# Two stacked transformer blocks on one core: three kinds of 16-bit turns by transposing transfers instead of TensorE

## What is computed

```python
xn = _layernorm(x)
x = x + L0_attn(xn, Wq, bq, Wk, bk, Wv, bv, Wo, bo) + L0_ffn(xn, w_gating, w_linear)
xn = _layernorm(x)
x = x + L1_attn(xn, wq, wk, wv, wo, inv_freq) + L1_ffn(xn, w_gate_up, w_proj)
# L0_attn: 32 query heads of width 8, 8 key/value heads, rotary, causal over the 1024 rows
# L0_ffn:  gelu(xn8 @ Wg0) * (xn8 @ Wg1), then @ w_linear, operands rounded to 8-bit floats
# L1_attn: rotary, softmax over the 16 heads of one row (each row by itself)
# L1_ffn:  ternary-quantized weights, silu(gate) * up, rms_norm, then @ w_proj
```

## Time and profile before

| | us |
|---|---|
| median of 3 runs | 600.06 |
| lowest, highest | 599.37, 602.33 |
| profiled execution: span, first to last instruction | 601.7 |
| profiled execution: its own time | not given, only the span is |
| TensorE, ScalarE, VectorE, GpSimd busy | 562.0, 469.6, 426.6, 233.6 |
| mean granted TensorE clock, share of full | 0.983 |

### The profile page before, as it was taken

The page is one execution under the profiler, slowest core; times in us unless marked ns, Lnnn a source line. Parts: engine busy times, 40 slices in busy tenths (PEclk is TensorE's granted clock), DMA queues, the critical chain, the costliest instruction groups (busy, mean ns, idle before and its releaser), DMA issues. The chain is left out here.

```text
span 601.7 us, 13300 instructions
## 1 busy us (share of the span) xinstructions
PE 562.0 (93%) x5153; PEld 290.7 (48%) x5153; DVE 426.6 (71%) x909; ACT 469.6 (78%) x607; POOL 233.6 (39%) x302
## 2 busy tenths in 40 slices
...
GB/s 265 303 36 2 36 1 35 36 2 49 6 62 33 33 59 39 27 37 3 19 17 2 64 54 27 89 55 27 54 10 36 45 20 69 17 68 85 94 57 48
DMA packets 150914, 30.40 MB, mean 51 GB/s; under 512 B 133952, under 2 KB 149568, under 8 KB 150848
## 3 DMA queue, kind: packets, MB, share of 16 engines
q1 hardware_dynamic: 150272, 29.19, 24.4%
q10 hardware_dynamic: 576, 0.33, 0.3%
...
## 5 line engine op out<-in xcount | busy, mean ns | idle before, releaser
L958 ACT ACTIVATE Pt<-psS 128x1024 f32<-128x1024 f32 x288 | 281.7, 1047 | 44.8 <-PE psS L685 25.9
L699 PE MATMUL psV<-Pt,vaug 128*32 128x512 f32 x1152 | 150.3, 611 | 0.3 <-POOL Pt L1645 0.3
L1645 POOL TENSOR_SCALAR_AFFINE_SELECT Pt<-Pt 128x1024 f32<-128x1024 f32 x64 | 71.7, 1145 | 43.8 <-ACT Pt L958 43.8
L685 PE MATMUL psS<-qTf,kTf 32*128 32x512 f16 x576 | 74.9, 390 | 7.3 <-ACT Pt L958 3.7
L685 PEld LDWEIGHTS psS<-qTf,kTf 32*128 32x128 f16 x576 | 20.3, 91 | 82.9 <-ACT Pt L958 48.1
L1695 POOL TENSOR_TENSOR ss<-ss,mhalf 128x1 f32<-128x1 f32 x16 | 9.5, 596 | 111.3 <-DVE ss L1476 111.3
L699 PEld LDWEIGHTS psV<-Pt,vaug 128*32 128x32 f32 x1152 | 25.7, 109 | 41.9 <-issue 35.9
L1016 ACT ACTIVATE stage<-psS 128x1024 f32<-128x1024 f32 x32 | 31.0, 1020 | 8.1 <-PE psS L821 7.9
L1686 POOL TENSOR_TENSOR r<-qk,cos 128x256 f32<-128x256 f32 x16 | 11.9, 744 | 63.9 <-ACT qk L991 58.0
L866 PE MATMUL psB<-wguT,xhs 128*128 128x512 bf16 x108 | 27.8, 380 | 0.0
L1032 ACT ACTIVATE qtmp<-qtmp 128x1024 bf16<-128x1024 f32 x16 | 16.9, 1059 | 12.9 <-PE psA L876 8.4
...
## 6 DMA issues: line engine op xcount, KB each, us to landing
qkvscr<-rqkv SPq DMA_DIRECT2D x16, 384.0 KB, 2.5
G<-qkvscr SPq DMA_DIRECT2D x24, 128.0 KB, 3.7
stage<-in_wg SPq DMA_DIRECT2D x4, 512.0 KB, 8.8
w8g<-qkvscr SPq DMA_DIRECT2D x16, 128.0 KB, 3.8
oscr<-o SPq DMA_DIRECT2D x16, 128.0 KB, 3.3
at<-oscr SPq DMA_DIRECT2D x16, 128.0 KB, 2.0
out<-yout SPq DMA_DIRECT2D x16, 128.0 KB, 2.5
...
```

Source lines behind the costliest of these rows:

```text
L685: e.matmul(psS[j], kd[32 * j:32 * j + k, h, 128 * at:128 * at + 128], qd[32 * j:32 * j + k, 4 * h:4 * h + 4, :].rearrange("p s n -> p (s n ...
L699: ins = e.matmul(psV[32 * j:32 * j + 32, :], vaug[:, at, j, 32 * h:32 * h + 32], Pt[(4 * Q + j) % NP], start=(kb == 0 and h == 0), stop=(k ...
L958: e.activation(flat(Pt4[:, u % NP:u % NP + 2, :]), flat(psS4[:, j:j + 2, :]), ACT.Exp, scale=scale).then_inc(S["exp"], 1)
L1645: e.affine_select(out=p, in_=p, pattern=[[0, 8], [1, 128]], compare_op=ALU.is_ge, fill=0.0, base=0, channel_multiplier=-1).then_inc(S["mas ...
```

## The change

`qxT`, `kTc`, `qTc`, `hxT`, `hTc` go, and `xn1T`, `xn1Tc` go from the first pass. Four transposing transfers on SP's queue replace them, from SBUF to SBUF: `kt`, `qt` (out of `QX`), `ht` (out of `hx_b`) and `xt`. For `xt` the split into a 16-bit part and its remainder is made ahead of the turn: a new VectorE step `xs` writes both into `xs_b`, memory that the first pass did not use. The steps that waited for a turn on TensorE or a copy on VectorE wait for a landing instead. The five lists of `ORDER` are all new (only SP's is shown); PSUM banks follow from TensorE's list.

```diff
     "sp": (
-        "wt.2 wg.2 wg.3 wg.4 wg.5 wt.3 wt.4 wt.5 vw.0 vr.0 vw.1 vr.1 ow.0 at1r.0 vw.2 vr.2 vw.3 ow.1 at1r.1 out.0 "
...
-        "at1r.12 vw.15 out.11 ow.13 vr.15 at1r.13 ow.14 out.12 at1r.14 ow.15 at1r.15 out.13 out.14 out.15"),
+        "wg.2 wg.3 qt.0 kt.0 qt.1 kt.1 wg.4 qt.2 wg.5 kt.2 qt.3 wt.2 kt.3 wt.3 qt.4 wt.4 xt.0 wt.5 kt.4 qt.5 xt.1 vw.0 "
+        "kt.5 kt.6 vr.0 qt.6 ht.0 xt.2 vw.1 xt.3 vr.1 ow.0 at1r.0 vw.2 vr.2 ht.1 qt.7 kt.7 ow.1 vw.3 at1r.1 vr.3 xt.4 "
...
+        "at1r.10 vw.12 vr.12 ht.11 xt.14 ow.11 vw.13 at1r.11 vr.13 ht.12 xt.15 vw.14 out.10 ow.12 vr.14 at1r.12 vw.15 "
+        "ow.13 vr.15 at1r.13 out.11 ht.13 ow.14 ht.14 out.12 out.13 at1r.14 ow.15 at1r.15 ht.15 out.14 out.15"),
...
+        xs_b = [flat(b[:]).bitcast(F16) for b in xn1T_b]
...
+            def kt(n):
+                at = n % NT % RING
+                w.wait_ge("q0", n + 1)
+                w.wait_ge("kl", n + 1)
+                w.wait_ge("pv", keys_free(n))
+                e.dma_start_transpose(kT[:, :, 128 * at:128 * at + 128],
+                                      QX[n % len(QX)][:, 32:40, :].rearrange("p h c -> p (h c)")).then_inc(S[f"d_kt{n % 2}"], 16)
+
+            def qt(n):
+                w.wait_ge("qh", n + 1)
+                w.wait_ge("ql", n + 1)
+                if n >= len(qT):
+                    w.wait_ge("qk", 4 * QUAD_END[n - len(qT)])
+                e.dma_start_transpose(qT[n % len(qT)],
+                                      QX[n % len(QX)][:, 0:32, :].rearrange("p h c -> p (h c)")).then_inc(S[f"d_qt{n % 2}"], 16)
+
+            def xt(n):
+                dst = xhs[n % len(xhs)]
+                w.wait_ge("xs", 2 * n + 2)
+                w.wait_ge("qkv1", 2 * (n + 1 - len(xhs)))
+                w.wait_ge("gu", 4 * (n + 1 - len(xhs)))
+                e.dma_start_transpose(dst[:].rearrange("p a (c n) -> p (a c) n", n=128),
+                                      xs_b[n % len(xs_b)]).then_inc(S[f"d_xt{n % 2}"], 16)
+
+            def ht(n):
+                w.wait_ge("hxa", n + 1)
+                w.wait_ge("hx", n + 1)
+                w.wait_ge("dn1", n)
+                w.wait_ge("wsum", 2)
+                e.dma_start_transpose(hT.rearrange("p k s n -> p (k s) n"),
+                                      hx_b.rearrange("p k n -> p (k n)")).then_inc(S["d_ht"], 16)
...
             def qk(Q):
-                    w.wait_ge("kTc", n - n % NB + kb + 1)
-                    w.wait_ge("qTc", n + 1)
+                    key = n - n % NB + kb
+                    w.wait_ge(f"d_kt{key % 2}", 16 * (key // 2 + 1))
+                    w.wait_ge(f"d_qt{n % 2}", 16 * (n // 2 + 1))
...
             def dn1(n):
-                w.wait_ge("hTc", 2 * n + 2)
+                w.wait_ge("d_ht", 16 * (n + 1))
...
             def qh(n):
-                    w.wait_ge("qxT", 2 * (n + 1 - len(QX)))
+                    w.wait_ge(f"d_qt{n % 2}", 16 * (n // 2))
...
             def ssq(n):
-                w.wait_ge("hxT", 2 * n)
+                w.wait_ge("d_ht", 16 * n)
...
+            def xs(n):
+                src, dst = xn1_b[n % len(xn1_b)], xs_b[n % len(xs_b)]
+                w.wait_ge("xn1", n + 1)
+                w.wait_ge(f"d_xt{n % 2}", 16 * (n // 2))
+                e.tensor_copy(dst[:, 0:256], src[:]).then_inc(S["xs"], 1)
+                w.wait_ge("xs", 2 * n + 1)
+                e.tensor_tensor(dst[:, 256:512], src[:], dst[:, 0:256], ALU.subtract).then_inc(S["xs"], 1)
```

More of the change, by code:

```diff
@@ L49 @@
     "pe": (
[48 rows of a table removed]
-    "act": (
[26 rows of a table removed]
-    "dve": (
[42 rows of a table removed]
-    "pool": (
[16 rows of a table removed]
[41 rows of a table added]
+    "act": (
[25 rows of a table added]
+    "dve": (
[37 rows of a table added]
+    "pool": (
[19 rows of a table added]
 }
 ROUND = {
[3 rows of a table removed]
[2 rows of a table added]
     "act": "qh QUADS g:0 fh:0 sq:0 th:0 g:1 fh:1 sq:1 th:1 qk1c gTk ex1 tg:0 tg:1 ssq hxa",
[5 rows of a table removed]
[4 rows of a table added]
 }
-PARTS = {"qxT": 2, "fxT": 3, "fTc": 3, "mT": 2, "up": 4, "qkv1": 2, "gT": 2, "gu": 4, "hxT": 2, "sq": 2, "fh": 2, "th": 2,
+PARTS = {"fxT": 3, "fTc": 3, "mT": 2, "up": 4, "qkv1": 2, "gT": 2, "gu": 4, "sq": 2, "fh": 2, "th": 2,
          "tg": 2, "mTc": 2, "g": 2, "ge1": 2, "ge3": 2, "sg": 2,
-         "hh": 2, "hTc": 2, "ge4": 2}
-ROUND2 = {e: r.replace("qxT:0 qxT:1", "fxT:0 fxT:1 fxT:2 rmm mT:0 mT:1").replace(" kl kTc qTc", " fTc:0 fTc:1 fTc:2 rmax mTc:0 mTc:1")
-          .replace(" ql", "").replace(" osum", "") for e, r in ROUND.items()}
+         "hh": 2, "ge4": 2}
 QUAD_STAGES = {"pe": ("qk", "pv"), "act": ("exp",), "pool": ("mask",)}
@@ L215, in one_round @@
     steps = []
-    for word in (ROUND if n < NT else ROUND2)[engine].split():
+    for word in ROUND[engine].split():
         if word == "QUADS":
@@ L236 @@
     "xnT": lambda n: ("xnTc", 2 * n + 2), "qkv": lambda n: ("qkvc", n + 1),
-    "qxT": lambda m: ("qTc" if m % 2 else "kTc", m // 2 + 1), "fxT": lambda m: ("fTc", m - 3 * NT + 1),
+    "fxT": lambda m: ("fTc", m - 3 * NT + 1),
     "mT": lambda m: ("mTc", m - 2 * NT + 1), "obT": lambda n: ("att", 2 * n + 2), "attT": lambda n: ("attTc", n + 1),
     "wo0": lambda n: ("xa", n + 1), "up": lambda m: ("fh" if m % 2 else "g", m // 2 + 1), "down": lambda n: ("yff", n + 1), "flagT": lambda n: ("flag", 1), "wsum": lambda m: ("wmin", m + 1),
-    "xn1T": lambda n: ("xn1Tc", 2 * n + 2) if n < NT else ("xn1f", n - NT + 1), "qkv1": lambda m: ("v1c" if m % 2 else "qk1c", m // 2 + 1),
+    "xn1T": lambda n: ("xn1f", n - NT + 1), "qkv1": lambda m: ("v1c" if m % 2 else "qk1c", m // 2 + 1),
     "gT": lambda m: ("gTk" if m % 2 else "gTq", m // 2 + 1), "gTagain": lambda n: ("gTm", n - NT + 1),
@@ L243 @@
     "o1T": lambda n: ("o1", 2 * n + 2), "at1T": lambda n: ("at1Tc", n + 1), "wo1": lambda n: ("yo", n + 1),
-    "gu": lambda m: ("hh" if m % 2 else "sg", m // 2 + 1), "hxT": lambda m: ("hTc", m + 1), "dn1": lambda n: ("yout", n + 1),
+    "gu": lambda m: ("hh" if m % 2 else "sg", m // 2 + 1), "dn1": lambda n: ("yout", n + 1),
     "ts": lambda m: ("tsc", m + 1), "td": lambda m: ("tde", m + 1), "tr": lambda m: ("tw", m + 1),
@@ L265, in score_banks @@
     return dict(zip(fills[1:], fills))
-SEMS = """d_x0 d_x1 d_x2 d_id d_b d_cs d_w0 d_c d_w1 d_wg0 d_wg1 d_gu0 d_gu1 d_vw0 d_vw1 d_vr d_ow d_or d_out0 d_out1
-xnT qkv qxT fxT mT obT attT wo0 up down xn1T qkv1 gT S1m gTagain S1 PV1 o1T at1T wo1 gu hxT dn1 ts td tr qk pv rmm flagT
+SEMS = """d_ht d_kt0 d_kt1 d_qt0 d_qt1 d_xt0 d_xt1 d_x0 d_x1 d_x2 d_id d_b d_cs d_w0 d_c d_w1 d_wg0 d_wg1 d_gu0 d_gu1 d_vw0 d_vw1 d_vr d_ow d_or d_out0 d_out1
+xnT qkv fxT mT obT attT wo0 up down xn1T qkv1 gT S1m gTagain S1 PV1 o1T at1T wo1 gu dn1 ts td tr qk pv rmm flagT
 qh exp g sq fh th qk1c gTk ex1 tg ssq hxa tc tde sin
-idc vz tab cst w8 w8m w8s tsc tm tcs tw ln0 xn xnTc qkvc va wide q0 kl kTc qTc fTc rmax rcomb mxn mTc ob att attTc xa ge1 ge3 ge3b a8c yff
-wh wsq wsum ln1 xn1 xn1Tc xn1f wl wmin v1c ro1 ro2 gTq m1 gTm o1r o1 sg hh ssm hx hTc at1Tc yo yout osum flag rng rngb
+idc vz tab cst w8 w8m w8s tsc tm tcs tw ln0 xn xnTc qkvc va wide q0 kl xs fTc rmax rcomb mxn mTc ob att attTc xa ge1 ge3 ge3b a8c yff
+wh wsq wsum ln1 xn1 xn1Tc xn1f wl wmin v1c ro1 ro2 gTq m1 gTm o1r o1 sg hh ssm hx at1Tc yo yout osum flag rng rngb
 zero gz zf rs0 rope ql mask ge4 xf rs1 ro1p rsg w8a""".split()
@@ L546, in all_landed @@
                 w.wait_ge("d_or", 16 * NT * passes)
-            run = {"wg": wg, "wt": wt, "vw": vw, "vr": vr, "ow": ow, "at1r": at1r, "out": out}
+                w.wait_ge("d_ht", 16 * NT * passes)
+            run = {"wg": wg, "wt": wt, "vw": vw, "vr": vr, "ow": ow, "at1r": at1r, "out": out, "kt": kt, "qt": qt, "xt": xt, "ht": ht}
             load_first()
@@ L626, in qkv @@
                 e.matmul(bank[:, 0:384], src[:, 1, :], wqkv[:, 1, :], start=False, stop=True).then_inc(S["qkv"], 1)
-            def qxT(m):
-                n, part = divmod(m, 2)
-                src = QX[n % len(QX)]
-                w.wait_ge("idc", 2)
-                w.wait_ge("q0", n + 1)
-                w.wait_ge("kl", n + 1)
-                if part == 1:
-                    w.wait_ge("qh", n + 1)
-                    w.wait_ge("ql", n + 1)
-                bank = shared("qxT", m)[:].bitcast(F16).rearrange("p (s n) -> p s n", n=128)
-                for at, u in enumerate(range(8) if part else range(8, 10)):
-                    ins = e.transpose(bank[:, at, :], src[:, 4 * u:4 * u + 4, :].rearrange("p r c -> p (r c)"), identh[:])
-                ins.then_inc(S["qxT"], 1)
             def transpose_heads(bank, units, sem):
@@ L769, in qkv1 @@
                     src = xhs[n % len(xhs)]
-                    w.wait_ge("xn1Tc", 2 * n + 2)
+                    w.wait_ge(f"d_xt{n % 2}", 16 * (n // 2 + 1))
                     w.wait_ge("wh", 1)
@@ L859, in gu @@
                 src = xhs[n % len(xhs)]
-                w.wait_ge("xn1Tc", 2 * n + 2)
```

(42 more changed lines are left out.)

19 lines of the change are left out of this document (8 added, 11 removed), and 260 rows, old and new, of tables (ORDER, ROUND).

## The result

The kernel after takes **570.01 us** (median of 4 runs, 569.08 to 571.85), the kernel before 599.73 on the same chip: ratio **0.951 [0.948, 0.954]**. Forecast were 579 us and a range of 558 to 601; the gain is 30 us where 21 were forecast.

A forecast was written before the change was run, and what follows sets the result against it. TensorE's queue was taken as the bound, above all from 150 to 540 us. 601.7 - 25 (turns) - 1 (copies) - 1 (holding) + 3 (start) + 3 (tail) = 580.7, less 1.6: 579 us, range 558 to 601.

The forecast's parts named there:

- TensorE's turns: Turns removed from TensorE's queue: 27.4 us, less 2.4 for those before 150 us where TensorE is not always the bound.
- VectorE's copies: 37.6 us of copies removed from VectorE: worth nothing from 150 us on, 1 us from 60 to 150.
- the chain's price: What a batch of turns costs its successor on TensorE, 0.45 us for 8; all removed turns sum to 27.4 us.
- the busy price: Removed turns priced by TensorE's busy time instead, 42 us in all; kept as the other end.
- The order: The new order of all five queues, priced at nothing, within plus or minus 3 us.
- less holding beside GpSimd: VectorE operations held while GpSimd runs: 15 us estimated in all, covered by TensorE after 150 us, counted as 1 us.
- Start and tail: Added cost of first `qt`, `kt` landing behind loads, 3 us (-1 to 8), and of last `ht`, 3 us (0 to 8).
- The rival in which they become the bound: Transposing transfers in 32-byte pieces fill the 16 engines; slower, 630 to 650 us; chance 0.10.
- From a landing of 6 us on, each us more is lost there: Single `hx` buffer at the last two tiles, 8.3 us apart; `dn1`, issue and landing make 7.3, which still fits.
- more than the sum: Rival: TensorE's turns are worth 42 us and less VectorE load shortens waits before 150 us; 561 us; chance 0.11.
- half is given back: Rival: transfers stand behind others on SP and TensorE waits, or start and tail cost most; 590 us; chance 0.17.
- the relief is eaten: Rival: ScalarE, full from 60 to 150 us, holds the rest; 597 to 603 us; chance 0.06.

The follow-up runs named there:

- run 6: The kernel after with 38 us of reductions added on VectorE and 28 unread turns in each down-projection (448) on TensorE: 605.8 us, 1.007 of the kernel before.
- run 5: The kernel after with 38 us of unread reductions added on VectorE, after `kl` and after `hx`: 589.1 us, 0.979 of the kernel before.
- run 7: The kernel before, own order, with VectorE's copies of turned matrices shrunk to 16 columns once buffers are filled; TensorE unchanged: 601.0 us, 0.997.
- runs 2 and 3: The kernel after with 16, then 48, unread turns added in each down-projection on TensorE (256 and 768): 582.1 and 608.7 us.
- run 1: The kernel before in its old order, all three kinds of turns replaced by transposing transfers: 623.2 us, 1.039 of the kernel before.
- run 8: The kernel before, own order, copies shrunk to 16 columns and 300 of 416 16-bit turns left out, no transfers: 594.8 us, 0.988.
- run 12: The kernel after with only its start reordered, so that the first keys and scores come earlier: 572.7 us, 0.950 of the kernel before.
- run 11: The kernel after with each `ht` transfer issued twice, the second after the first has landed: 623.8 us, 1.037 of the kernel before.

## Why the prediction was right, and where it was not

The sum of the prediction can be set beside runs that give each part back, in the new order:

| term | forecast, us | measured, us | from |
|---|---|---|---|
| TensorE's turns | -25 | -17 to -21 | run 6 less run 5; 448 turns at 0.047 |
| VectorE's copies | -1 | -17 to -13 | run 5 less the kernel after; run 6 less the 448 turns |
| the two together | -26 | -34 | run 6 less the kernel after |
| order, start, tail, transfers | +5 | +4 | run 6 less the kernel before |
| all | -21 | -30 | |

The first two terms share some microseconds: the one that is given back first costs more. The time fell inside the forecast's band partly by luck, since one term was too dear by 4 to 8 us and the other too cheap by 12 to 16.

- **VectorE: the step that failed.** "VectorE has slack where TensorE is the bound, so this is worth nothing from 150 on; TensorE hides it." It holds in the old order (1.7 us, run 7) and not in the new one, where 38 us cost 17. 125 free us of 390 say how much VectorE is not doing, not that its steps can be late: in run 5 TensorE's idle time from 150 to 510 went from 3 to 13 us with VectorE busy for 254 of 360. The prediction took the old order's slack and read it into a kernel with five new lists, and so put a term of 13 to 17 us at 1.
- **TensorE: right in kind, a sixth to a third too dear.** The batch's price from the chain, 0.45 us for 8, gives 0.056 a turn; a turn in the new order costs 0.037 to 0.047. The choice of the chain's price over the busy price (0.079) was right; 42 us would have been far off. Between runs 2 and 3 TensorE's busy time itself grows by only 0.055 us a turn, the chain's price: the 0.079 of the rows counts what overlaps with neighbours. In the old order a turn is worth 0.018. (The 32 turns of `xn1`, in fp32, are counted here like the others.)
- **The order: priced at "nothing, within plus or minus 3".** As a lone term that is what run 6 shows (+4 with start, tail and transfers in it). But it isn't a term by itself: relief in the old order gives +23 us with transfers (in my placing, all of it behind the last scores) and -7 without them, for two thirds of the load (runs 1 and 8), the new order with the old load +4, both together -30. The gain is that of the pair. The prediction had no case for this, and had the old order been kept, as in run 1, its 579 would have been wrong in sign. The 1 us for less holding beside GpSimd has no sign in the trace: with 37.6 us of copies gone VectorE's busy time falls by 31.7, and `xn` takes 579 ns at the median against 408.
- **Start and tail: right numbers, other causes.** They came at +3.6 and +3.4 us of TensorE's idle time against +3 and +3. For the start the reason given, the first scores, was not the cause: they were 7.6 us later (29.8 against 22.2, inside 24 to 30), and taking 4.4 of these back changed nothing (run 12). For the tail the reason given was the landing of `ht`, but there TensorE never waits for it directly (ScalarE does once, 8.2 us); its longest waits are for the attention output's way through DRAM, 5.2 us from 510 us on against 2.5 from 540 us on in the kernel before, and the chain that ended last runs through that transfer. From the last scores to the end both kernels take about the same, 68.4 and 68.8 us. The longest of these waits in the kernel after:

```profile
PE psB L610 <- DMA at<-oscr: 2.9, 2, 1.7
```

- **Transfers: hidden, but not as said.** All landing times are at the cheap end. The rival in which they become the bound is out: 40.9% of the 16 engines. By the Trainium skill, page "VectorE: DVE Perf Modes", section "The three transpose paths", a 128x128 turn by the crossbar costs 1309 ns. As a price for each block the trace disagrees, since `ht` turns 16 blocks in 3.8 us with its issue, 0.24 us a block at most; the smallest, `kt`, turns 2 in 2.6 us, so it is the first blocks that are dear. The prediction's second figure, 2 us for `ht` beyond the fixed part, was the nearer one: from 128 to 512 KB the landing grows by 1.2 us.
- **The waits.** "From a landing of 6 us on, each us more is lost there", at the last two tiles. Run 11 has it lost all along, at 7.4 us from the first issue to the second landing: 3.2 us a tile, some 0.9 us for each of the 3.7 us more, TensorE's lower clock included. The average distance of 28 us between tiles was no measure of the slack, because SP's line and `ssq` on ScalarE hold other tiles' work behind one late `ht`.

Three of the rivals' mechanisms exist, then: "more than the sum" for its second reason (VectorE), "half is given back" as soon as transfers come 4 us later or the order does not allow for them, and, as far as the scores' rows of run 8 show, "the relief is eaten" by ScalarE in the old order.

What stays open: why the new order needs VectorE's time where the old did not. Run 5 shows that TensorE then stands, not which of the two places (after `kl` or after `hx`) does it; the two were not tried apart.
